# A selective scan pipelined over four engines: row folds a quarter unit later, spreads first, two products from VectorE to GpSimd

## The reference, cut to what matters

```python
x = x + _L1_conv_ref(_ln_c(x), ...)      # Mamba on 8x8 windows
t = _to_tokens(x)
t = t + _L1_ffn_ref(_ln_t(t), ...)       # experts: only its norm and logits are made here

def _ln_c(v, eps=1e-06):                 # (v - mean) / sqrt(var + eps) over the channels
    ...
def _mamba(xw, ...):
    xz = seq @ W_in;  x, z = split(xz)
    x = silu(causal_conv(x) + conv_b)    # u in the kernel
    dt, Bm, Cm = split(x @ W_xproj)
    dt = softplus(dt @ W_dt + b_dt)
    # h = exp(dt*A)*h + (dt*u)*B ; y = sum_n h*C + u*D   for 16 states n
    y = y * silu(z)
    return y @ W_out
```

## Time and profile before

| what | value |
|---|---|
| median of 3 runs | 9768.39 us |
| the profiled execution, its own time | 9759.82 us |
| its span, first to last instruction | 9758.0 us |
| DVE busy over the span | 6949.3 us (71%) |
| PE busy | 6743.3 us (69%) |
| POOL busy | 5336.3 us (55%) |
| ACT busy | 4390.8 us (45%) |
| mean granted TensorE clock | 0.795 of full speed |

### The profile page before, as it was taken

The page is one execution under the profiler, slowest core; times in us unless marked ns, Lnnn a source line. Parts: engine busy times, 40 slices in busy tenths (PEclk is TensorE's granted clock), DMA queues, the critical chain, the costliest instruction groups (busy, mean ns, idle before and its releaser), DMA issues. The chain is left out here.

```text
span 9758.0 us, 102749 instructions
## 1 busy us (share of the span) xinstructions
PE 6743.3 (69%) x30290; PEld 2778.7 (28%) x30290; DVE 6949.3 (71%) x7923; ACT 4390.8 (45%) x5988; POOL 5336.3 (55%) x2619
## 2 busy tenths in 40 slices
PE   6888888888866666666666666666666666666644
PEld 3444444444431211212111221112112111211133
DVE  3555555555548888888888888888888888888833
ACT  1222222222225555565565565555556555555500
POOL 0000000000018888888888888888888888888700
PEclk8888888888877777777777777777778777777766
DMA  0000000000015444545544554454445455444454
GB/s 19 20 18 18 20 20 16 20 20 18 18 60 177 162 162 170 179 160 172 182 160 164 174 175 161 170 179 162 161 170 181 162 171 179 162 162 170 146 149 137
DMA packets 494003, 1202.18 MB, mean 123 GB/s; under 512 B 166501, under 2 KB 168713, under 8 KB 493705
## 3 DMA queue, kind: packets, MB, share of 16 engines
q1 hardware_dynamic: 493449, 1201.14, 36.7%
q0 software_dynamic: 512, 0.53, 0.0%
HBM read 943.43 MB, written 231.21 MB: 120 GB/s over the span
## 5 line engine op out<-in xcount | busy, mean ns | idle before, releaser
L983 POOL TENSOR_TENSOR b_h<-b_h,b_ct 128x896 f32<-128x896 f32 x1792 | 3704.9, 2086 | 888.6 <-DVE b_h L1140 879.7
L1140 DVE TENSOR_TENSOR_SCAN b_h<-b_a,b_h 128x448 f32<-128x448 f32 x3584 | 3678.0, 1073 | 572.5 <-ACT b_a L1068 560.2
L1068 ACT ACTIVATE b_a<-b_dts,decay 128x441 f32<-128x441 f32 x3584 | 2212.8, 629 | 1318.0 <-DVE b_h L1140 1303.4
L1251 PE MATMUL b_y<-b_h,fold 128*32 128x512 f32 (+1 forms) x7168 | 1076.5, 734 | 1100.8 <-POOL b_h L983 1100.8
L1130 DVE TENSOR_TENSOR b_h<-b_dus,b_b 128x896 f32<-128x896 f32 x1344 | 1434.4, 1067 | 494.6 <-PE b_b L1243 447.9
L990 POOL MEMSET b_seq<- 128x938 f32 x2 | 1.7, 880 | 2768.0 <-POOLq L768 2768.0
L1243 PE MATMUL b_b<-b_rows,spread_b 16*128 16x512 f32 (+1 forms) x1792 | 741.0, 835 | 583.3 <-DVE b_h L1130 581.7
L472 DVE TENSOR_TENSOR a_xg<-a_xn,a_pb 128x784 f32<-128x784 f32 x512 | 495.9, 969 | 629.4 <-PE a_pb L586 629.4
L971 POOL TENSOR_TENSOR b_h<-b_dus,b_bt 128x896 f32<-128x896 f32 x448 | 932.6, 2082 | 13.3 <-DMA b_dus<-d_dtu 10.5
L595 PE MATMUL a_pa<-a_xg,w_exp 128*128 128x512 f32 (+1 forms) x2048 | 927.3, 580 | 0.0
L1251 PEld LDWEIGHTS b_y<-b_h,fold 128*32 128x32 f32 x7168 | 222.0, 130 | 1780.0 <-POOL b_h L983 1311.5
(11 more groups left out here) (209 smaller groups left out, 8506.9 us busy)
## 6 DMA issues: line engine op xcount, KB each, us to landing
b_bt<-d_rows SPq DMA_DIRECT2D x448, 448.0 KB, 6.1
b_ct<-d_rows SPq DMA_DIRECT2D x448, 448.0 KB, 3.8
b_dts<-d_dt SPq DMA_DIRECT2D x448, 448.0 KB, 5.8
b_dus<-d_dtu SPq DMA_DIRECT2D x448, 448.0 KB, 5.6
d_dt<-b_dt SPq DMA_DIRECT2D x112, 448.0 KB, 2.5
d_dtu<-b_soft SPq DMA_DIRECT2D x112, 448.0 KB, 2.7
b_seq<-b_seq SPq DMA_DIRECT2D x112, 234.0 KB, 4.5
a_x<-in_x SPq DMA_DIRECT2D x64, 392.0 KB, 3.2
```

The lines of the kernel that those rows point to most:

```text
L983: nc.gpsimd.tensor_tensor(hh[t][:], hh[t][:], ct[t // 4 % 2][:], ALU.mult).then_inc(hc_done, 1)
L1068: a(steps(bank(aa, k)), steps(half(dts[t % 4], k)), ACT.Exp, scale=decay[:, t % 4, t // 4:t // 4 + 1]).then_inc(a_done, 1)
L1140: v.tensor_tensor_scan(half(hh[t], k), bank(aa, k), half(hh[t], k), 0.0, ALU.mult, ALU.add).then_inc(h_done, 1)
L1251: last = mm(yy[32 * b:32 * b + 32, lo:hi], fold[:], hh[4 * row + b][:, lo:hi], start=False, stop=(row == 3))
```

## The change

```diff
 # GpSimd
+                        def norm(c, o):
+                            pool.wait_ge(rstd_ready, o + 1)
+                            pool.wait_ge(moved, c + 2)
+                            nc.gpsimd.tensor_tensor(xc[:], xc[:], sq[:], ALU.mult).then_inc(xn_ready, 1)
+                        def final_norm(c, q):
...
+                            nc.gpsimd.tensor_tensor(xl[:], xl[:], sq2[:], ALU.mult).then_inc(xl_ready, 1)
...
+                                if t == 4 and i == 0 and kind != LAST:
+                                    norm(spot(0, "xc", it, kind), it + 1)
+                                if t == 4 and i == 1 and kind != FIRST:
+                                    final_norm(spot(1, "xc2", it, kind), it - 1)
 # ScalarE
-                                if t == 6 and more:
+                                if t == 5 and more:
...
                                     softplus_start(spot(i, "pre", it, kind))
-                                if t == 7 and more:
+                                if t == 6 and more:
                                     softplus_end(o + 1)
-                                if t == 9 and more:
+                                if t == 8 and more:
...
                                     move(spot(i, "xp", it, kind), rows[1 - i][:], rows=4 * NS)
-                                if t == 12 and more:
+                                if t == 10 and more:
...
                                     move(spot(i, "z", it, kind), gate[1 - i][:])
-                                if t == 14 and finals:
+                                if t == 12 and finals:
...
                                     move(spot(1, "lgp", it, kind), lg[:], ACT.Identity, rows=2 * EC, bias=b_gate[:])
-                                if t == 15 and finals:
+                                if t == 14 and finals:
...
                                     move(spot(1, "tok", it, kind), tok[:])
 # VectorE: norm, final_norm and their calls at t == 5 are gone
 # TensorE
-                            if not (kind == FIRST and i == 0):
-                                fold_row(3, tile_no(i, 15, it) - UNIT)
+                            if not first:
+                                fold_row(2, tile_no(i, 11, it) - UNIT)
...
                                 conv(spot(i, "conv", it, kind), 1 - i, it + i)
+                            if not first:
+                                fold_row(3, tile_no(i, 15, it) - UNIT)
+                            if more:
                                 strip(spot(i, "pre", it, kind), w_dt_full[:], u[1 - i])
+                            skip_start(i, unit_no(i, it))
                             spread_row(2, i, it)
-                            skip_start(i, unit_no(i, it))
...
                             fold_row(0, tile_no(i, 3, it))
-                            fold_row(1, tile_no(i, 7, it))
-                            spread_row(3, i, it)
                             if more:
                                 gate_in(spot(i, "z", it, kind), 1 - i)
+                            spread_row(3, i, it)
...
                                 final_products(spot(1, "lgp", it, kind), it - 1)
+                            fold_row(1, tile_no(i, 7, it))
+                            if finals:
                                 transposes(spot(1, "tok", it, kind))
-                            fold_row(2, tile_no(i, 11, it))
...
+                        fold_row(2, tile_no(1, 11, N))
                         fold_row(3, tile_no(1, UNIT - 1, N))
```

More of the change, by code:

```diff
@@ L948, in products @@
                             nc.gpsimd.tensor_tensor(soft[:], dtb[:], u[j][:], ALU.mult).then_inc(dtu_ready, 1)
+                        def norm(c, o):
[3 more added lines that the diff above has]
+                        def final_norm(c, q):
+                            pool.wait_ge(rstd2_ready, q + 1)
+                            pool.wait_ge(moved, c + 2)
+                            nc.gpsimd.tensor_tensor(xl[:], xl[:], sq2[:], ALU.mult).then_inc(xl_ready, 1)
                         def sequences(c, o, last):
@@ L991, in _ @@
                         pool.wait_ge(pads_zero, 2)
+                        norm(START.index("xc"), 1)
                         sequences(None, 1, None)
@@ L996, in _ @@
                         turns(unit)(pool)
+                        final_norm(spot_final("xc2"), N)
                     @block.scalar
@@ L1150, in scan_before @@
                                 scan(UNIT - 1, 1, it - 1)
[L1152 to L1155, removed]
                         def gated(j, row, o):
@@ L1167, in residual @@
                             v.tensor_tensor(win(x3s), seqs(ww), win(xr), ALU.add).then_inc(moved, 1)
[L1169 to L1172, removed]
                         def unit(i, it, kind):
@@ L1181, in unit @@
                                     gated(1 - i, row_no(i, 0, it) - 1, unit_no(i, it) - 1)
[L1182 to L1185, removed]
                                 if t == 14 and i == 0 and kind != FIRST:
@@ L1189, in _ @@
                         v.memset(aa[:], 0.0).then_inc(aa_zero, 1)
-                        norm(START.index("xc"), 1)
                         turns(unit)(dve)
@@ L1194, in _ @@
                         residual(spot_final("out"), N)
-                        final_norm(spot_final("xc2"), N)
                     @block.tensor
@@ L1284, in unit @@
                             finals = i == 1 and kind != FIRST
+                            first = kind == FIRST and i == 0
                             spread_row(0, i, it)
```

## The result

The changed kernel takes 8927.38 us, the median of 4 runs (8923.87 to 8933.02), against 9770.41 us for the kernel before (4 runs). The ratio is 0.9135, with an interval of 0.9119 to 0.9151.

What follows compares the result with a forecast made beforehand. Engines' waits for one another, not a full engine, bound the kernel. Turns falling from 113.9 to 99.3 us save 774 over 53, plus 22 outside, less 21 stray: 9759.8 - 775 = 8985, plus 8.6 for the median, 8994; range 8945 to 9270.

Steps and rivals of the forecast that it cites:

- A ring of waits: Phase B, 113.9 us a turn: no engine is full; late POOL delays folds, then TensorE, ScalarE and DVE, then POOL again.
- The case given 0.64: Main case: POOL becomes the fed bound at 99.3 us a turn, 8994 us in all, own range 8950 to 9080.
- The floor of a turn: Phase B: POOL's work 95.2 us plus 4.1 for the products, 99.3; DVE's 91.0 plus its waits, 96.0.
- the 0.4 us a turn for stray waits: Set against the gain in phase B's 53 turns: 21 us in all.
- The turns outside the stretch: First and last turns outside the 53 profiled ones, three in number: they run emptier, half of their 44 us gained, 22.
- The low end of the range: 8945 us, of a range to 9270 that takes in the main case, passed-on waits and TensorE as bound.
- the lag: End of POOL's last tile of a unit less end of DVE's last scan: about 9 us before, settling near 9.5.
- its limit of 11.1: `gated` needs fold 3 at D + 14.3: no cost up to a lag of 11.1 us, one for one beyond.
- ScalarE's own late work: DVE waits a unit for exponentials: 0.4 us after the logarithm, 0.9 at the silus, 1.2 at softplus_end.
- become the bound: Rival, chance 0.10: TensorE's matmuls, all at half clock, take 104 us a turn; 9233 us in all.
- the rival in which the wait only moves: Chance 0.05: with lag above 11 us, `gated` waits for fold 3; 108 us a turn, 9450 in all.
- The slower rival: Chance 0.04: ScalarE's six earlier moves wait as z did, each holding DVE 4.0 us; 120 a turn, 10,100 in all.

## Why the prediction was right, and where it was wrong

- **What bounds the kernel: right.** A ring of waits. Fold 3 back in its place costs 488 us, fold 1 back 427, and with both moved GpSimd's waits of the earlier trace rows are gone.
- **GpSimd becomes the bound and never waits: right.** 99.5% busy, 2.5 us of waits for scans in 53 turns. The case given 0.64 is the one that came, though the time lies 23 us below that case's own range.
- **The floor of a turn: mis-sized, and this is the step that failed.** I took GpSimd's work as the stretch less its named waits, 95.2 us "with the small gaps that stay", and with 4.1 for the two products got 99.3. It was 98.8, of which 98.3 work and 0.5 gaps. The small gaps did stay: the time without work beside the named waits was 1017.0 - 993.7 = 23.3 us before and 26.4 - 2.5 = 23.9 after. What shrank is the work. An instruction of GpSimd between two waits counts 2.08 us of busy time; in a row without waits each starts 2.04 us after the one before it, so six count 12.30. With some 720 waits in the stretch, its 2439 instructions took 5020.49 / 2439 = 2.058 us each; after, 5208.85 / 2546 = 2.046. Over the 2439 instructions that is 0.6 us a turn. The plain busy time of the earlier trace rows plus 4.1 also gives 98.8, but by luck: it is 0.5 us too high for the work (98.3 was measured) and leaves out the gaps, 0.5 us.
- **The other small terms, all against me.** My sum has the stretch at 6037.5 - 774 + 21 = 5284.5 us; it was 5235.2. Of these 49 us, 28 are the floor and 21 the 0.4 us a turn for stray waits, which did not come. The turns outside the stretch gave 28 where I took 22. The median lies 2.5 us below the profiled execution, where I added 8.6: another 11. That makes 66 of the 67 us between 8994 and 8927.
- **The low end of the range: wrong.** With 98.8 us a turn and no stray waits my own terms give 9759.8 - 800 - 22 + 8.6 = 8946. So 8945 was that floor with the two small terms as I had them, and left them no room. With all 44 us outside the stretch and nothing added for the median it would have been 8916.
- **The price of the products on GpSimd, 4.1 us a turn: right.** Both lines take 2.09 us in the middle.
- **The rule against this part** (the Trainium skill, GPSIMD Engine Reference, "Engine selection", which puts elementwise products on VectorE): I noted that the products on VectorE would leave GpSimd below 94.9 and VectorE 4.4 us longer. Both kernels were run: on VectorE it is 218 us slower. My 4.4 was itself too small, since 2.2 us was the price beside a GpSimd that soon ran dry; in the new order the two take 4.0 and 2.7 in the middle, and GpSimd still waited for scans.
- **What holds VectorE back: wrong place, no cost.** I had the lag settle near 9.5 us by the load of dus(2) behind `sequences`. That wait is 17.5 us in all. VectorE is held by GpSimd's product of tile 0, which `scan` 0 needs, 142.9 us, and by `gated`, 133.0. I had named `gated` and its limit of 11.1; the other I had not seen. All 53 of these waits are for tile 0 of the odd unit. Its product stands ahead of GpSimd's tile 13 of the even unit, and four operations (8.1 us) follow it there. VectorE asks for it 1.0 us after its last scan, so it waits once the lag is over 9.1. Here the lag was 11.9 (6096.6 to 6108.5) and VectorE waits 2.84:

```profile
6098.30 2.10 POOL L981 TENSOR_TENSOR b_h<-b_dus,b_bt 128x896 f32<-128x896 f32 x1
...
6100.52 2.07 DVE L1156 TENSOR_TENSOR_SCAN b_h<-b_a,b_h 128x448 f32<-128x448 f32 x2 [2.84 <-POOL b_h L981]
```

- **ScalarE's own late work: right in kind, half the size.** VectorE waits 127.9 us in all for exponentials, 2.4 a turn where I had 5.0. Softplus_end leaves 0.88 us in every unit where I had 1.2. The silus leave 0.87 in the middle, but in 27 of the 53 even units and as good as never in the odd ones, and tile 3's waits come to 9.5 us. As GpSimd is the bound, this moved no time.
- **The rivals.** TensorE did not become the bound: its clock rose from 0.77 to 0.81 in the stretch and it was busy 69.4 us a turn. VectorE waits 133.0 us before `gated`, the sign of the rival in which the wait only moves, but GpSimd has work in hand and the time stays. The slower rival did not come, because z no longer waits behind fold 1. With that order back its mechanism came, at 9893 us where the rival had 10,100.

## What to carry to other kernels

When no engine is full, find the ring: follow one wait from the dry engine back until it meets that engine again, and move whatever waits for the late engine behind all that feeds it. Once the ring is open, the turn is the longest engine's instructions at the pace that they have one behind the other, plus its small gaps. Take that pace from a row without waits: 48 instructions a turn at 2.044 us by the earlier trace rows and 0.4 us of gaps make 98.6, and 98.8 was measured, while busy time counted among waits was too long. Put the low end of a range where every small term is at its best.

A part can do nothing or harm in one surrounding and pay in another: ScalarE's earlier steps cost 310 us in the old order, nothing in the new one, and gain 78 once VectorE is nearly full too. So judge the parts together with the one that opens the ring.

## What the hardware showed that I had not expected

A product of two SBUF tensors on VectorE does not simply wait for the GpSimd instruction that runs when it is issued. With its norm products on VectorE, the new order shows two outcomes in its 112 products. In 74 the product ended with GpSimd idle, and 64 of these let one or two instructions pass that GpSimd began after it; the longest took 6368 ns, where the shortest took 1092. In the other 38 it came in between two instructions of GpSimd, and the second took 2.93 us instead of 2.08. What decides between the two was not found. With one operand in PSUM the product took 1078 ns in the middle beside a GpSimd as busy.
